# Expert layers whose outputs leave TensorE with stream positions along the columns, added to the stream from PSUM

## The reference, cut to what matters

```
x = x + attention0(cond0(x))
x = x + expert0(cond1(x))     # gate MLP with layer norm, top 2 of 8 LoRA experts with a capacity
x = x + attention1(cond2(x))
x = x + expert1(cond3(x))     # softmax router, top 2 of 8 LoRA experts, and a bias

# both expert layers, for n tokens of 512 features
h    = x @ A                    # 8 experts, rank 16: 128 values for each token
hw   = h * (weights of the chosen experts)
out  = x @ W.T + hw @ B * scale (+ b_base in expert1)
```

## Time and profile before

| | |
|---|---|
| median of the runs | 1037.94 us |
| lowest | 1037.42 us |
| the profiled execution, its own time | 1035.93 us |
| its span, first to last instruction | 1033.9 us |
| mean granted TensorE clock | 0.983 |

### The profile page before, as it was taken

The page is one execution under the profiler, slowest core; times in us unless marked ns, Lnnn a source line. Parts: engine busy times, 40 slices in busy tenths (PEclk is TensorE's granted clock), DMA queues, the critical chain, the costliest instruction groups (busy, mean ns, idle before and its releaser), DMA issues.

```text
span 1033.9 us, 15771 instructions
## 1 busy us (share of the span) xinstructions
PE 971.3 (94%) x6686; PEld 698.4 (68%) x6686; DVE 555.3 (54%) x951; ACT 229.8 (22%) x443; POOL 456.2 (44%) x413
## 2 busy tenths in 40 slices
PE   5899989999999999999998889989999998799997
PEld 2338877778888788877886669639745555445853
DVE  7866738484474837657385334425248687102323
ACT  4601022221202121211111100110253646300001
POOL 7936548583767727496574303103113335300300
PEclk9999999999999999999999899999999999799999
DMA  5782102001111101111103290874520000540002
GB/s 134 181 235 67 54 10 101 8 37 52 42 72 42 51 1 41 72 41 52 42 3 120 59 233 6 180 146 166 204 102 2 2 3 2 112 113 1 3 1 82
DMA packets 36286, 74.29 MB, mean 72 GB/s; under 512 B 13492, under 2 KB 22260, under 8 KB 33140
## 3 DMA queue, kind: packets, MB, share of 16 engines
q1 hardware_dynamic: 35880, 72.89, 25.5%
q10 hardware_dynamic: 336, 0.39, 0.1%
HBM read 66.26 MB, written 7.01 MB: 71 GB/s over the span
## 4 chain that ended last, share of the span: by engine, by line
PE 74%; DVE 10%; POOL 7%; ACT 4%; issue 3%; DMA 1%; SPq 0%; POOLq 0%; DVEq 0%; ACTq 0%
PE ps L1186 15%; PE ps L1124 14%; PE ps L992 8%; PE ps L1425 5%; PE ps L1253 5%; PE ps L1357 5%; PE ps L1138 4%; POOL w_lo L2277 3%; DVE arena L1951 3%; ACT acts L1457 2%; PE ps L1258 2%; DVE arena L1948 1%; DVE h_lo L1960 1%; PE ps L1384 1%; PE ps L1378 1%
## 5 line engine op out<-in xcount | busy, mean ns | idle before, releaser
L2378 POOL TENSOR_TENSOR arena<-arena 128x512 f32<-128x512 f32 x80 | 103.6, 1295 | 122.7 <-DVE arena L1951 122.5
L1124 PE MATMUL ps<-xt_hi,w_hi 128*128 128x512 f32 x320 | 127.7, 399 | 5.5 <-POOL w_lo L2277 2.7
L1124 PE MATMUL ps<-xt_lo,w_hi 128*128 128x512 f32 x320 | 125.7, 393 | 0.0
L1124 PE MATMUL ps<-xt_hi,w_lo 128*128 128x512 f32 x320 | 125.0, 391 | 0.0
L1186 PE MATMUL ps<-h_hi,wo_hi 128*128 128x512 f32 x256 | 105.2, 411 | 11.9 <-DVE h_lo L1960 11.9
L2300 POOL TENSOR_TENSOR xt<-arena 128x512 f32<-128x512 f32 x24 | 30.5, 1271 | 190.7 <-DVE arena L1854 190.7
L1969 DVE TENSOR_TENSOR fresh<-ps,fresh 128x512 f32<-128x512 f32 x56 | 38.7, 692 | 136.0 <-PE ps L1186 135.9
L1951 DVE TENSOR_TENSOR arena<-ps,rope 64x512 f32<-64x512 f32 x160 | 110.2, 689 | 2.2
L1186 PE MATMUL ps<-h_lo,wo_hi 128*128 128x512 f32 x256 | 103.7, 405 | 0.0
L1186 PE MATMUL ps<-h_hi,wo_lo 128*128 128x512 f32 x256 | 103.1, 403 | 0.0
L1550 ACT ACTIVATE h_hi<-ps 128x512 fp32r<-128x512 f32 x64 | 33.1, 604 | 204.4 <-PE ps L1171 204.4
(11 more groups left out here) (311 smaller groups left out, 1807.0 us busy)
## 6 DMA issues: line engine op xcount, KB each, us to landing
acts<-in_w_o_dram SPq DMA_DIRECT2D x8, 1024.0 KB, 5.0
arena<-in_a_wo_dram SPq DMA_DIRECT2D x8, 1024.0 KB, 5.8
arena<-kernel_rows SPq DMA_DIRECT2D x11, 512.0 KB, 12.0
acts<-in_w_qkv_dram SPq DMA_DIRECT2D x3, 1792.0 KB, 7.2
acts<-in_w_qkv_dram SPq DMA_DIRECT2D x4, 1280.0 KB, 6.7
w_l<-kernel_rows SPq DMA_DIRECT2D x10, 512.0 KB, 12.0
arena<-level_rows SPq DMA_DIRECT2D x4, 1024.0 KB, 22.0
stream<-in_x_dram SPq DMA_DIRECT2D x4, 512.0 KB, 6.9
```

What stands on the lines that cost most here:

```text
L1124: last = pe.matmul(ps[:, bank, :], w[:, r, cols], x, start=(r == 0 and n == 0), stop=(r == R - 1 and n == 2))
L2378: pool.tensor_tensor(qk[:, chunk, half * HALF:(half + 1) * HALF], rot[:, k % 2, 0, :], rot[:, k % 2, 1, :], ALU.add).then_inc(s_rope, 1)
```

## The change

The expert layers' outputs are made in the stream's own layout. `main(k)` now covers group k of four samples: for each sample j and each residue r, the 32 tokens of the sample are stationary and the weights [128 t, 128 t_out] of each r_out move, into partitions 32*r_out to 32*r_out+31, columns j*128 onward. `lora(k)` does the same with the LoRA values. VectorE's `ffn` adds each bank to the stream directly (`s_added`), for eight groups; the copies to `fresh` by ScalarE and VectorE, and the turns and `add_back` of stages 1 and 3, are gone. `conv(2)` waits for 1, 2, 5 and 8 additions ahead of its groups 0 to 3, the last two since it reuses banks 0, 2 and 3.

The bias of layer 1 can no longer be one value for each partition: POOL, after its part of `conv(3)`, broadcasts it into 128 columns (`bias_cols`), TensorE turns that with four matmuls ahead of the token products, ScalarE copies it (`bias_rows`), and POOL adds it to the stream in eight additions, each of which VectorE's addition of the group waits for. On SP's queue the three loads of attention 1 now wait for the turns of stage 0, and the first two wo loads for the additions of stage 1.

```diff
--- before.py
+++ after.py
@@ -314,6 +314,7 @@
         keys_n = sp3.take(NTILE, 2 * ROT)
         tmp_k = sp3.take(2, NTILE, QA)
         lat_n = tmp_k[:, 1].rearrange("p m (k l) -> p m k l", k=G)
+        bias_cols, bias_rows = late[:, 0, 0:R * C], late[:, 1, 0:P]
         f1_main = w_l0[:, NSPARE:NSPARE + R * R * P].rearrange("p (a r t) -> p a r t", a=R, r=R)
         rank_const = sb("rank_const", [P, NE])
         ones = sb("ones", [P, P])
@@ -560,8 +561,10 @@
         s_lturn = [sem(f"ffn{n}_lora_turned") for n in range(2)]
         s_lcopy = [sem(f"ffn{n}_lora_copied") for n in range(2)]
         s_ffn = [sem(f"ffn{n}_output_tile_done") for n in range(2)]
-        s_fact = [sem(f"ffn{n}_act_copied") for n in range(2)]
-        s_fdve = [sem(f"ffn{n}_dve_copied") for n in range(2)]
+        s_bcols = sem("ffn1_bias_columns_ready")
+        s_bturn = sem("ffn1_bias_turned")
+        s_brows = sem("ffn1_bias_rows_ready")
+        s_badd = sem("ffn1_bias_added")
 
         s1_w = sem("l1_arena_weights_loaded")
         s1_wm = sem("l1_factor_weights_loaded")
@@ -858,10 +861,11 @@
             sp.dma_start(rope1r, a["rope1r"]).then_inc(s1_w, 16)
             sp.dma_start(rope1c, a["rope1c"]).then_inc(s1_w, 16)
 
-            sp.wait_ge(s_back[1], NGROUP)
+            sp.wait_ge(s_back[0], NGROUP)
             sp.dma_start(w_nope, a["a1_nope"]).then_inc(s1_wm, 16)
             sp.dma_start(w_kb, a["a1_kb"]).then_inc(s1_wm, 16)
             sp.dma_start(w_v, a["a1_v"]).then_inc(s1_wm, 16)
+            sp.wait_ge(s_added[1], NGROUP)
             for i in range(2):
                 sp.dma_start(wo1[i], a["a1_wo"][i]).then_inc(s1_wo[i], 16)
             patch(2)
@@ -1041,18 +1045,18 @@
 
             def conv(net, half_ready, all_ready):
 
-                turns = {0: (0, 1, 2, 3), 1: (4, 5), 2: (6, 7)}
+                turns = {0: (0, 1, 2, 3), 1: (4, 5), 2: (6, 7)} if net % 2 else {}
                 for g in range(NGROUP):
                     for what, count in {0: half_ready, 1: all_ready}.get(g, ()):
                         pe.wait_ge(what, count)
-                    for t in turns.get(g, ()) if net else ():
+                    for t in turns.get(g, ()):
                         turn(net - 1, t)
                     if g == 0:
                         pe.wait_ge(s_kern[net], 16 * 13)
                         if net == 0:
                             pe.wait_ge(s_cev, NCMP * NET)
                     if net:
-                        pe.wait_ge(s_added[net - 1], g + 1)
+                        pe.wait_ge(s_added[net - 1], (1, 2, 5, 8)[min(g, 3)] if net == 2 else g + 1)
                     elif g % 2 == 0:
                         pe.wait_ge(s_stream[g // 2], 16)
                     if net == 0:
@@ -1244,19 +1248,33 @@
                     conv(net, ((s_fresh, 8 * NKV - 4),), ((s_fresh, 8 * NKV),))
                 else:
                     conv(net, ((s1_oact, 2), (s1_odve, 2)), ((s1_oact, 4), (s1_odve, 4)))
+                if n:
+                    pe.wait_ge(s_bcols, 1)
+                    for r in range(R):
+                        last = pe.matmul(ps[32 * r:32 * r + 32, 6, 0:P], bias_cols[:, r * C:(r + 1) * C], ident[:, :],
+                                         start=True, stop=True)
+                    last.then_inc(s_bturn, 1)
                 for m in range(NTILE):
                     token_products(m)
 
                 def main(k):
-                    half, r_out = k // 4, k % 4
-                    for r in range(R):
-                        pe.matmul(ps[:, FFN_BANK[k], :], w_main[:, r, r_out, :],
-                                  xt[:, r, half * HALF:(half + 1) * HALF], start=(r == 0), stop=False)
+                    if n and k == 2:
+                        pe.wait_ge(s_brows, 1)
+                    for j in range(G):
+                        toks = slice((k * G + j) * C, (k * G + j + 1) * C)
+                        for r in range(R):
+                            for r_out in range(R):
+                                pe.matmul(ps[32 * r_out:32 * r_out + 32, FFN_BANK[k], j * P:(j + 1) * P],
+                                          xt[:, r, toks], w_main[:, r, r_out, :],
+                                          start=(j == 0 and r == 0), stop=True, skip_group_check=True)
 
                 def lora(k):
-                    half, r_out = k // 4, k % 4
-                    pe.matmul(ps[:, FFN_BANK[k], :], w_out[:, r_out, :], lora_t[:, half * HALF:(half + 1) * HALF],
-                              start=False, stop=True).then_inc(s_ffn[n], 1)
+                    for j in range(G):
+                        toks = slice((k * G + j) * C, (k * G + j + 1) * C)
+                        for r_out in range(R):
+                            last = pe.matmul(ps[32 * r_out:32 * r_out + 32, FFN_BANK[k], j * P:(j + 1) * P],
+                                             lora_t[:, toks], w_out[:, r_out, :], **ADD)
+                    last.then_inc(s_ffn[n], 1)
 
                 for k in range(6):
                     if k >= 4:
@@ -1312,7 +1330,7 @@
                                          wo1[i % 3][:, g, :], start=True, stop=True)
                     last.then_inc(s1_wc, 1)
 
-                conv(2, ((s_fact[0], 2), (s_fdve[0], 2)), ((s_fact[0], 4), (s_fdve[0], 4)))
+                conv(2, (), ())
                 pe.wait_ge(s1_wm, 48)
 
                 for i in range(8):
@@ -1430,12 +1448,6 @@
             ffn(0)
             attention1()
             ffn(1)
-            for g in range(NGROUP):
-                for what, count in {0: ((s_fact[1], 2), (s_fdve[1], 2)),
-                                    NGROUP // 2: ((s_fact[1], 4), (s_fdve[1], 4))}.get(g, ()):
-                    pe.wait_ge(what, count)
-                turn(3, g)
-
 
         @block.scalar
         def _(act):
@@ -1565,6 +1577,9 @@
 
             def ffn(n):
                 width = (NAT0, NAT1)[n]
+                if n:
+                    act.wait_ge(s_bturn, 1)
+                    act.activation(bias_rows, ps[:, 6, 0:P], ACT.Copy).then_inc(s_brows, 1)
                 for q in range(4):
                     act.wait_ge(s_nat[n], q + 1)
                     act.activation(nat[:, 2 * q:2 * q + 2, 0:width],
@@ -1582,13 +1597,6 @@
                     act.wait_ge(s_lturn[n], q + 1)
                     act.activation(lora_t[:, q * HALF:(q + 1) * HALF], ps[:, 2 + q, :], ACT.Copy)\
                         .then_inc(s_lcopy[n], 1)
-                for k in range(0, 8, 2):
-                    half, r_out = k // 4, k % 4
-                    act.wait_ge(s_ffn[n], k + 1)
-                    act.activation(fresh[:, half * 16:half * 16 + 16, r_out, :],
-                                   ps[:, FFN_BANK[k], :].rearrange("p (b c) -> p b c", c=C),
-                                   ACT.Identity, bias=f1_bias[:, 0, r_out:r_out + 1] if n else 0.0)\
-                        .then_inc(s_fact[n], 1)
 
             def attention1():
                 def copy_projection(q):
@@ -1896,9 +1904,9 @@
                     for layer in range(3):
                         scaled_tiles(3, (range(4), range(4, 8), range(8, 13))[layer])
                         edge_values(0, layer)
-                adds = {0: (0, 1, 2, 3), 1: (4, 5), 2: (6, 7)}
+                adds = {0: (0, 1, 2, 3), 1: (4, 5), 2: (6, 7)} if net % 2 else {}
                 for g in range(NGROUP):
-                    for k in adds.get(g, ()) if net else ():
+                    for k in adds.get(g, ()):
                         add_back(net - 1, k)
                         if k == 0 and net in (1, 3):
                             zero_edge_pads()
@@ -2122,16 +2130,13 @@
 
             def ffn(n):
                 (gate0, gate1)[n]()
-                for k in range(1, 8, 2):
-                    half, r_out = k // 4, k % 4
+                for k in range(NGROUP):
                     dve.wait_ge(s_ffn[n], k + 1)
-                    dst = fresh[:, half * 16:half * 16 + 16, r_out, :]
-                    src = ps[:, FFN_BANK[k], :].rearrange("p (b c) -> p b c", c=C)
                     if n:
-                        last = dve.tensor_scalar(dst, src, f1_bias[:, 0, r_out:r_out + 1], None, ALU.add)
-                    else:
-                        last = dve.tensor_copy(dst, src)
-                    last.then_inc(s_fdve[n], 1)
+                        dve.wait_ge(s_badd, k + 1)
+                    x = stream[:, k * G:(k + 1) * G, 1:T + 1]
+                    dve.tensor_tensor(x, ps[:, FFN_BANK[k], :].rearrange("p (b t) -> p b t", t=T), x, ALU.add)\
+                        .then_inc(s_added[2 * n + 1], 1)
 
             def attention1():
                 dve.wait_ge(s1_w, 112)
@@ -2220,8 +2225,6 @@
             attention1()
             conv(3)
             ffn(1)
-            for g in range(NGROUP):
-                add_back(3, g)
 
 
         @block.gpsimd
@@ -2431,6 +2434,15 @@
             kernel_zeros(3, 2)
             conv(3)
 
+            pool.wait_ge(s_fw[1], 64)
```

(8 more changed lines are left out.)

## The result

The changed kernel takes 1046.99 us (median of four; 1046.01 to 1047.78) against 1038.18 us for the one before: a ratio of 1.0087, 95% interval 1.0067 to 1.0107. It is slower by about 9 us where 7 us less were forecast. The profiled execution took 1046.6 us with a span of 1044.8 us.

The account below looks back on a forecast made before the run. TensorE, busy 94% of the span, was taken as the bound. Layer 0 with stage 2 (-3.5 us) and layer 1 (-3.85) made -7.3 us, from 1037.94 to 1030.6 us, range 1026.5 to 1043.

Parts of the forecast that it names:

- Part 1: Expert layers' products in four column tiles: 640 matmuls at 54.5 ns, 34.9 us, 0.6 us more for each layer.
- rival C: Tiled matmuls don't keep 54.5 ns over a run of 384; at 63.8 ns +4.5 us, 1042.4 us; chance 0.12.
- D: Rival: instruction feed slower still, 80 ns a matmul in both layers, 1063 us; chance 0.03.
- Part 2: Stage 2's convolution without turns: 26.5 us from layer 0's last LoRA to the first projection, a gain of 4.1 us.
- The clock: Low clock on layer 0's six LoRA matmuls, 7.02 us against 5.42 in layer 1: the 1.6 us kept as unchanged.
- Part 3: Start of layer 1: TensorE waits for POOL's bias copy ahead of the token products, net +2.65 us on the path.
- Rival B: The wait for the bias lowers the clock, costing 1.6 us on layer 1's token products: 1032.2 us; chance 0.1.
- Part 4: Behind layer 1's last LoRA only one addition and one output DMA remain: end at 1026.8 us, a gain of 7.1 us.
- The range: 1026.5 to 1043 us overall; low end from the 53.3 ns pace (-1.6) and 1.6 us of clock saved.

Follow-up runs that it names:

- the fastest version: Layer 0 as before, layer 1 as changed, bias turned behind the token products, layer 0's counting matmul behind four mains instead of six: 1028.67 us, ratio 0.9911 to the kernel before.

## Why the prediction was wrong

**Part 1, the pace.** The sum took 54.5 ns for every one of the 640 matmuls in either layer. In layer 1 that held: 21.10 us for 384 is 54.9 ns. In layer 0 it was 97 ns. That all of it is on the path was right. The step that failed is the pace, "A run of 640 pays the fixed part hardly ever, so I take 54.5 ns", which was read from bursts of 32 matmuls and took nothing for the instructions' own way to TensorE. In its place the runs showed a wait for instruction blocks behind the loads: 12.3 us of gaps, 2.75 us of low clock between them, +16.7 us for the six mains where +0.35 was forecast. A burst of 128 instructions lies within half a block, so it can't show what a block costs. The text named "the stream of 2,560 instructions a layer running dry" as half of rival C, and priced it by a steady pace, the same in both layers; it didn't ask what feeds the stream, although the page of the kernel before lists the instruction queue among the DMA queues, and although the DMA engines were full in exactly these 20 us. The chance of C and D, 0.15, was far too low, and C's 1042.4 us too small: the mains alone lost 16.4 us in one layer.

The Trainium skill, "Runtime: NRT & Kernel Launch", section "Instruction fetch mechanics", says that instructions are refilled in 16 KiB blocks of 256 over a DMA queue of the sequencer's own, and that crossing a block costs little, mostly hidden. The pieces of 128 matmul records with their 128 weight loads are that block, as this trace shows it; the cost is hidden in layer 1 and isn't in layer 0, where the gaps are 0.57 to 5.79 us. There the measurement decides.

**Part 2, stage 2 without turns.** Right: 26.3 us against 26.5, a gain of 4.3 against 4.1. SP's moved waits cost nothing in the changed kernel.

**The clock.** Kept at 1.6 us in layer 0, it was there again (the six LoRAs took 6.9 us, 7.0 before), and 2.75 us more inside the starved mains (granted clock 0.56 over that piece, behind the idle times of 2.85 and 5.79 us). The 3.0 us in attention 1 had no place in the sum: I took a stretch of unchanged code for one of unchanged time. Which work meets the low clock differs from version to version: these products took 55.2 us in six of the eleven profiles and 56.7 to 58.2 us in five. What decides it stays open.

**Part 3, the bias.** The idle time was 2.45 us (2.8 forecast), POOL's copy 0.29 us (0.42 taken). From conv(3)'s last matmul to the first main the stage took 10.5 us, 8.5 before: +2.0 us where +2.65 was forecast. Rival B's dip didn't come in the changed kernel's profile, and did in three versions with the same wait.

**Part 4, the end.** Right: the last LoRA ends near 1040.4 us, and 4.4 us later the kernel does; 4.6 were forecast. Layer 1 as a whole gained 4.0 us, 3.85 forecast, and part of that closeness is luck: the bias cost 0.65 us less than forecast and the products 0.7 us more (from the first main to the last LoRA's end 37.5 us in place of 36.2).

**The range.** Its low end doesn't follow from its own terms: 1030.6 less 1.6 and 1.6 us is 1027.4, not 1026.5. It changes nothing in the argument.

## What to carry to other kernels

Before a few long matmuls are cut into many short ones, count instructions as a load on the DMA engines, 64 bytes each (16 KB for 256): here 2,560 instructions a layer want a 16 KB block every 3.5 us, and beside full queues a block came up to 9.7 us behind the one before. Where such a form is worth it, put it where no bulk loads run; the same change gained 4 us in one layer and lost 12 in the other (16.7 of mains less 4.3 of turns), and only taking it where it pays, with the wait for the bias moved off the path, beat both kernels, by 0.5% (0.9% with the counting matmul moved too). A pace read from a burst holds for runs as long as that burst.

## What the runs showed that was not expected

In layer 1, gaps put down to "issue" of 0.20 to 0.85 us appear in seven of the versions, and each ends 1.2 to 1.6 us behind the landing of an instruction block. All but one (0.23 us) stand behind the first output store, so the stores may starve the new form a little; no run shows it. A wait of 2.45 us of TensorE is followed by half the clock in some profiles of versions with this wait and not in others. With layer 0 as before, the runs with the wait spread over 8.2 us, six without it over 2.4; but the changed kernel, which has it too, spreads over only 1.8 in four runs, the fastest version, without it, over 4.2, and eleven runs of the kernel before over 4.9. So the dip is seen, and what spreads the runs stays open. And beside POOL's additions over 128x512, VectorE's small operations with two inputs take four to five times as long, 0.86 and 1.12 us for 0.22, while its reductions keep their 0.22 us.
